# Down basis of a spline FFN in float32 on column halves of TensorE, with GpSimd rounding and a new order of the batch loop

## The chip, the cores and the metric

The kernel runs on one core of a Trainium2 chip. The metric is the device time of one execution in microseconds (us). PE is TensorE (the matrix engine), ACT ScalarE, DVE VectorE, POOL GpSimd, SP SyncE, which issues the DMAs. PE writes its products to eight PSUM banks of 128 x 512 float32.

## The reference, cut to what matters

Four batches, 512 tokens, width 512. Cross attention adds to x; then a gated FFN, whose three weight matrices are Catmull-Rom splines of few control points, adds to the result.

```python
# attention (per batch)
query, key = features @ Wq.T + bq, features @ Wk.T + bk
attention = softmax(query @ key.T)
x = x + layernorm(x) @ attention.T          # layernorm over the last axis
# FFN (per batch), INTER = 2048 rows
h = layernorm(x)
inter = silu(h @ gate_w.T) * (h @ up_w.T)
x = x + inter @ down_w.T                    # weights: spline_reconstruct(control points)
```

## The kernel before, in words

**Weights.** A spline matrix is, over most of its area, a smooth function, so each product with a weight matrix is split in two: a small basis part through nodes, and a residual with the breaks. For the down matrix the basis part is: `zd = d_u^T inter`, 128 node rows by 512 tokens, and then `zd` times `d_v` (the node weights). The residual is `d_r`, 16 tiles of 128 x 192 columns in blocks, times the rounded activations `ih`. The 2048 inner rows lie in 16 tiles m of 128; tile m = 4w + a touches only the node rows of class w.

**Precision.** PE takes float32r operands (rounded) in one pass and float32 in two recorded passes that are slower. To keep the precision of the basis product in float32r, both factors are split into a rounded part and a remainder: `d_u` is [P, 16, 2, 128] with high and low part, and an activation tile is `ih` (rounded, by ACT) and `il` (remainder, by POOL). Three products per tile (lines 1301, 1302, 1304) give `zd`.

**Order.** Every engine runs the same written list of stage calls (`attention_only`, then `ffn`), each with its own body for each stage, in strict order; semaphores join the engines. `ffn(b, a)` runs the FFN of batch b with the attention of batch a = b + 1 woven in; it is the body of a loop of three iterations, and then it runs once more for the last batch with no attention. The steps of a batch:

- `project`: basis coefficients `zg` of the normalised input (PE line 1273, ACT 775, DVE 950), and POOL's copy `xres` (line 1096).
- `gate_up(m)`: four products of 512 columns (lines 1287, 1289) into gbank[m % 2] and ubank[m % 2]. The gate part waits until tile m-2's SiLU has read its bank, the up part until its multiply has.
- `activate(m)`: ACT SiLU into one of three `inter` buffers (line 784), DVE multiply by the up result (line 958).
- `round_inter(m)`: ACT rounds `inter` to `ih[m]` (line 788), POOL computes `il` (line 1108).
- `down_basis(m)`: the three products above, accumulated in `zdbank`.
- `down(t, tiles)`: `ih[m]` times `d_r[m]` for 128 tokens (line 1318), 16 products for each of four t; `down_split` splits `zd` (ACT 795, DVE 968); `down_tail(t)`: `zd` times `d_v` (line 1325); DVE adds to `xres` (line 976), SP stores.
- attention of a: `qk` (PE 1150, float32; ACT 682), `energy(t)` (PE 1161, float32), `softmax(t)` (DVE maximum 849, ACT exp 694), `scale` (DVE reciprocal 853, four scalings 856), `prob_t(t)` (PE transposes 1204, all four need the scaled rows), `split_prob(t)` (ACT 714, DVE 879), `split_x` (ACT `xh` 720, DVE `xl` 883), `xm(t)` (PE 1247 to 1249, 12 products each), `add_xm`, `cast_t`, `norm_t` (PE 1262).

The energies and exps of the four row blocks stand together in the middle of the gate_up steps, after `activate` 8 and 9, and `down_basis` steps of earlier tiles stand between gate_up steps. SiLU and exp are in different ACT table sets; the compiler puts an ACT_TABLE_LOAD before the first function of another set. The prologue builds the weights; there `down_factors` splits the basis (ACT 748, DVE 923), POOL clears `d_u` (line 991), and `down_nodes` makes `d_v` (POOL 1055, DVE 896 to 901). In the prologue `node_weights` runs float32 products on strips of 32 rows (line 1225).

Of the kernel before, what the change touches and what calls it, by code (L numbers as in the profile page):

```python
# [49 lines left out]
LAG = 3  # L50
EARLY, FILL = 10, 3
HALF = 64
WIDTH = PERIOD / 4
# [77 lines left out]
def constants():  # L131
# [52 lines left out]
    at["d_node"] = np.repeat(idx[:, None], 2, 1).transpose(0, 1, 3, 2).reshape(P, 4, HID)  # L184
    c["d_coef"] = taps.transpose(0, 2, 3, 1).reshape(P, 4 * HID).astype(np.float32)
# [8 lines left out]
    for m in range(MT):  # L194
        w = m // CLS
        full, k = basis_at(tiles[m].astype(float), edges)
        at_cell = 8 * np.arange(D_LIVE // 4)[:, None] + 2 * w + np.arange(4)
        basis[:, m] = np.pad(full, ((0, 0), (0, 8)))[:, at_cell.ravel()]
# [15 lines left out]
def xattn_spline_ffn_kernel(nc: bass.Bass, d, out: bass.AP):  # L214
# [4 lines left out]
    with ctx:  # L219
# [18 lines left out]
        d_u = sb("d_u", [P, MT, 2, P], f32r)  # L238
# [40 lines left out]
        basis_f = sb("basis_f", [P, MT, D_LIVE], f32, prep)  # L279
# [12 lines left out]
        inter = sb("inter", [P, 3, TOK], f32)  # L292
        il = sb("il", [P, 2, TOK], f32r)
# [22 lines left out]
        def live(part, w):  # L316

            first, n = 2 * w, 16 if w + 1 < CLS else 15
            row = d_u[:, CLS * w:CLS * (w + 1), part]
            if w + 1 < CLS:  # L320
                return row.rearrange("p m (q e) -> p m q e", e=8)[:, :, :, first:first + 4]
            return row[:, :, first:first + 8 * n].rearrange("p m (q e) -> p m q e", e=8)[:, :, :, 0:4]

        def live_basis(w):

            n = 16 if w + 1 < CLS else 15
            return basis_f[:, CLS * w:CLS * (w + 1), 0:4 * n].rearrange("p m (q e) -> p m q e", e=4)

        def in_tiles(psum):
# [4 lines left out]
        zgbank, zdbank = bank[4], bank[5]  # L334
        abank = bank[6:8]
# [3 lines left out]
            consts_set warm_set du_zero win_hi win_split power_done node_mm node_hi node_done  # L339
            jump_sums jump_k2 jump_c jump_d jump_hi jump_split res_mm res_mul res_done  # L340
            dtap_mul dtap_sum dv_hi dv_done du_hi du_done
# [3 lines left out]
            x1_kept zg_mm zg_hi zg_done g_mm u_mm silu_done mult_done ih_done il_done zd_mm zd_hi zd_done  # L345
# [10 lines left out]
        def attention_only(st):  # L356
# [55 lines left out]
            st.down_factors()  # L412
# [44 lines left out]
        def ffn(st, b, a=None):  # L457

            st.project(b)
            for m in range(2):  # L460
                st.activate(b, m)
            st.round_inter(b, 0)
            st.activate(b, 2)
            st.round_inter(b, 1)
            st.activate(b, 3)
            st.round_inter(b, 2)
            if a is not None:
                st.qk(a)
            st.gate_up(b, 0)
            st.activate(b, 4)  # L470
            st.gate_up(b, 1)
            st.round_inter(b, 3)
            st.gate_up(b, 2)
            st.activate(b, 5)
            st.gate_up(b, 3)
            for m in range(4, 6):
                st.round_inter(b, m)
            st.down_basis(b, 0)
            st.activate(b, 6)
            for m in range(4, 6):  # L480
                st.gate_up(b, m)
            st.down_basis(b, 1)
            st.activate(b, 7)
            st.down_basis(b, 2)
            st.gate_up(b, 6)
            st.round_inter(b, 6)
            st.down_basis(b, 3)
            st.round_inter(b, 7)
            st.gate_up(b, 7)
            for m in range(8, 10):  # L490
                st.activate(b, m)
            st.down_basis(b, 4)
            st.gate_up(b, 8)
            if a is not None:
                for t in range(2):
                    st.softmax(a, t)
            st.round_inter(b, 8)
            st.gate_up(b, 9)
            if a is not None:
                st.energy(a, 0)  # L500
            st.round_inter(b, 9)
            if a is not None:
                st.softmax(a, 2)
                st.energy(a, 1)
                st.softmax(a, 3)
                st.scale(a)
            for m in range(5, 7):
                st.down_basis(b, m)
            st.activate(b, 10)
            if a is not None:  # L510
                st.energy(a, 2)
            st.activate(b, 11)
            if a is not None:
                st.split_prob(a, 0)
                st.energy(a, 3)
            st.down_basis(b, 7)
            st.gate_up(b, 10)
            st.down_basis(b, 8)
            st.gate_up(b, 11)
            st.down_basis(b, 9)  # L520
            st.round_inter(b, 10)
            if a is not None:
                st.prob_t(a, 0)
            st.gate_up(b, 12)
            if a is not None:
                st.prob_t(a, 1)
            st.gate_up(b, 13)
            st.activate(b, 12)
            if a is not None:
                st.prob_t(a, 2)  # L530
            st.down_basis(b, 10)
            st.gate_up(b, 14)
            if a is not None:
                st.prob_t(a, 3)
            st.gate_up(b, 15)
            if a is not None:
                st.split_prob(a, 1)
            st.down_basis(b, 11)
            st.round_inter(b, 11)
            st.down(b, 0, range(0, 13))  # L540
            st.activate(b, 13)
            if a is not None:
                st.split_prob(a, 2)
            st.round_inter(b, 12)
            for m in range(12, 14):
                st.down_basis(b, m)
            st.down(b, 0, range(13, 16))
            st.down(b, 1, range(0, 16))
            st.round_inter(b, 13)
            st.activate(b, 14)  # L550
            if a is not None:
                st.split_prob(a, 3)
                st.xm(a, 0)
            st.activate(b, 15)
            if a is not None:
                st.split_x(a)
            for m in range(14, 16):
                st.round_inter(b, m)
            if a is not None:
                st.stats(a)  # L560
            st.down_basis(b, 14)
            if a is not None:
                st.xm(a, 1)
            st.down_basis(b, 15)
            if a is not None:
# [36 lines left out]
        def _(sp):  # L602
# [24 lines left out]
            load(basis_f[:].rearrange("p m n -> p (m n)"), "d_basis", "dbasis_in")  # L627
# [35 lines left out]
        def _(act):  # L663
            class Stages:
# [104 lines left out]
                def project(b):  # L769
                    act.wait_ge(s["zg_mm"], b + 1)  # L770
                    if isinstance(b, int) and b == 0 or not isinstance(b, int):
                        act.wait_ge(s["res_done"], RES)
                        act.wait_ge(s["du_done"], CLS)
# [16 lines left out]
                def down_basis(b, m):  # L790
                    pass
# [568 lines left out]
```

## Time and profile before

| | |
|---|---|
| median of three runs | 295.74 us (295.48 to 298.01) |
| profiled execution, its span | 295.4 us |
| PE busy | 278.2 us (94%) |
| DVE, POOL, ACT busy | 179.8, 157.8, 153.9 us |
| chain that ended last, PE's share | 81% |
| DMA moved | 23.34 MB, mean 79 GB/s |

Matmuls are pipelined: a recorded duration (0.39 us for 512 columns) is longer than the distance from one start to the next (0.23 us). Distances between starts tell what PE can do.

### The profile page before, as it was taken

How to read it: one execution, taken by the hardware profiler on the slowest of the kernel's cores; microseconds unless marked ns; L12 is line 12 of the kernel's file. 1: busy time of each engine (PE TensorE's matmuls, PEld its weight loads, DVE VectorE, ACT ScalarE, POOL GpSimd, SP SyncE). 2: the span in 40 equal slices, each digit the busy share in tenths (PEclk: the TensorE clock that was granted, in tenths of full speed). 3: DMA queues.
4: the chain of work that ended last, by engine and by line, in shares of the span. 5: the costliest groups of instructions: out<-in, count | busy, mean ns of one | idle time of the engine just before them, and what ended most of it. 6: DMA issues, size and time to landing. Idle time of an engine off the chain costs nothing.

```text
span 295.4 us, 4068 instructions
## 1 busy us (share of the span) xinstructions
PE 278.2 (94%) x1298; PEld 199.5 (68%) x1300; DVE 179.8 (61%) x318; ACT 153.9 (52%) x259; POOL 157.8 (53%) x139
## 2 busy tenths in 40 slices
PE   8699489899999999999999999999999999799995
PEld 3132157654777888946868888657688888477894
DVE  1697988985466676743467856524677577343403
ACT  3044733224888923256899422458897132376710
POOL 5589252778565772225855723058547521598630
PEclk9958869999999999999999999999999999999999
DMA  7997044000900000036200000333000001100003
GB/s 204 376 426 290 0 124 163 0 2 0 354 3 0 3 0 2 21 121 237 118 0 0 0 0 0 142 118 166 0 0 0 0 0 71 71 0 3 0 0 144
DMA packets 7212, 23.34 MB, mean 79 GB/s; under 512 B 1185, under 2 KB 2337, under 8 KB 5793
## 3 DMA queue, kind: packets, MB, share of 16 engines
q1 hardware_dynamic: 7200, 23.20, 21.1%
q8 instruction: 6, 0.10, 0.1%
q14 instruction: 6, 0.04, 0.0%
HBM read 19.01 MB, written 4.19 MB: 79 GB/s over the span
## 4 chain that ended last, share of the span: by engine, by line
PE 81%; DVE 10%; DMA 2%; ACT 2%; POOL 2%; issue 1%; SPq 1%; DVEq 0%; POOLq 0%
PE bank L1287 11%; PE bank L1289 10%; PE bank L1318 10%; PE bank L1150 6%; PE bank L1304 5%; PE bank L1273 5%; PE bank L1301 5%; PE bank L1302 5%; PE bank L1325 4%; PE bank L1247 4%; PE bank L1248 4%; PE bank L1249 4%; PE bank L1161 3%; PE bank L1204 3%; DVE prod L872 2%; DMA power<-in_g_power 2%
## 5 line engine op out<-in xcount | busy, mean ns | idle before, releaser
L1108 POOL TENSOR_TENSOR il<-inter,ih 128x512 fp32r<-128x512 f32 x64 | 86.6, 1366 | 46.3 <-ACT ih L788 29.4
L958 DVE TENSOR_TENSOR inter<-inter,bank 128x512 f32<-128x512 f32 x64 | 43.6, 685 | 45.6 <-ACT inter L784 45.5
L784 ACT ACTIVATE inter<-bank 128x512 f32<-128x512 f32 x64 | 37.9, 596 | 17.0 <-PE bank L1289 14.4
L788 ACT ACTIVATE ih<-inter 128x512 fp32r<-128x512 f32 x64 | 39.3, 629 | 2.4 <-DVE inter L958 2.3
L759 ACT ACTIVATE qk<-bank,nmr,rstd 128x512 f32<-128x512 f32 x16 | 12.5, 779 | 40.0 <-PE bank L1249 22.5
L1318 PEld LDWEIGHTS bank<-d_r,ih 128*128 128x128 f32 x256 | 30.8, 191 | 2.1 <-ACT ih L788 1.0
L1318 PE MATMUL bank<-d_r,ih 128*128 128x192 f32 x256 | 31.1, 274 | 0.0
L1287 PE MATMUL bank<-xh,gate_r 128*128 128x512 f32 x64 | 27.3, 426 | 1.5 <-DVE zg L950 1.5
L1301 PE MATMUL bank<-ih,d_u 128*128 128x512 f32 x64 | 28.0, 437 | 0.0
L1096 POOL TENSOR_TENSOR xres<-x,ones 128x2048 f32<-128x2048 f32 x4 | 14.4, 3600 | 23.9 <-DMA out<-xres 23.6
L1287 PE MATMUL bank<-xh,up_r 128*128 128x512 f32 x64 | 25.6, 400 | 0.0
L1304 PE MATMUL bank<-il,d_u 128*128 128x512 f32 x64 | 25.2, 394 | 0.4 <-POOL il L1108 0.4
L1289 PE MATMUL bank<-zg,gate_v 102*128 102x512 f32 x64 | 25.4, 396 | 0.0
L1289 PE MATMUL bank<-zg,up_v 102*128 102x512 f32 x64 | 25.3, 395 | 0.0
L1247 PE MATMUL bank<-ph,xh 128*128 128x512 f32 x64 | 25.2, 394 | 0.0
L1302 PE MATMUL bank<-ih,d_u 128*128 128x512 f32 x64 | 25.2, 394 | 0.0
L1248 PE MATMUL bank<-pl,xh 128*128 128x512 f32 x64 | 24.9, 390 | 0.0
L1249 PE MATMUL bank<-ph,xl 128*128 128x512 f32 x64 | 24.9, 389 | 0.0
L1079 POOL TENSOR_TENSOR ve<-mv,eps 128x1 f32<-128x1 f32 x16 | 5.9, 369 | 33.7 <-DVE mv L935 33.7
L764 ACT ACTIVATE prob<-bank 128x512 f32<-128x512 f32 x16 | 8.7, 596 | 21.6 <-PE bank L1262 21.6
L1150 PE MATMUL bank<-ctxT,wqk 128*128 128x512 f32 x32 | 17.5, 696 | 0.0
L930 DVE TENSOR_TENSOR x<-x,qk 128x512 f32<-128x512 f32 x16 | 11.1, 694 | 9.7 <-ACT qk L759 9.7
(97 smaller groups left out, 519.3 us busy)
## 6 DMA issues: line engine op xcount, KB each, us to landing
x<-in_x SPq DMA_DIRECT2D x4, 1024.0 KB, 4.7
xT<-in_xT SPq DMA_DIRECT2D x4, 1024.0 KB, 7.0
out<-xres SPq DMA_DIRECT2D x16, 256.0 KB, 2.1
ctxT<-in_ctxT SPq DMA_DIRECT2D x4, 512.0 KB, 7.4
rd<-in_d_r SPq DMA_DIRECT2D x2, 768.0 KB, 6.2
knots<-in_d_knot SPq DMA_DIRECT2D x1, 1280.0 KB, 11.6
d_coef<-in_d_coef SPq DMA_DIRECT2D x1, 1024.0 KB, 14.9
d_pt<-in_d_node SPq DMA_DIRECT2D x1, 1024.0 KB, 17.5
```

The costliest lines, as they stand in the source:

```text
L784: nc.scalar.activation(inter[:, m % 3], gbank[m % 2][:], ACT.Silu).then_inc(s["silu_done"], 1)
L788: nc.scalar.activation(ih[:, m], inter[:, m % 3], ACT.Copy).then_inc(s["ih_done"], 1)
L958: V.tensor_tensor(inter[:, m % 3], inter[:, m % 3], ubank[m % 2][:], ALU.mult).then_inc(s["mult_done"], 1)
L1108: G.tensor_tensor(il[:, m % 2], inter[:, m % 3], ih[:, m].bitcast(f32), ALU.subtract).then_inc(s["il_done"], 1)
L1247: mm(abank[t % 2][:], xh[:, n, c], ph[:, n], start=n == 0, stop=False)
L1248: mm(abank[t % 2][:], xh[:, n, c], pl[:, n], start=False, stop=False)
L1287: mm(dst[m % 2][:], gu_r[n][:, a, w * P:(w + 1) * P], xn2r[:, a], start=True, stop=False)
L1289: mm(dst[m % 2][:], gu_v[n][:, m], zg[:], start=False, stop=True).then_inc(s[done], 1)
L1301: mm(zdbank[:], d_u[:, m, 0], ih[:, m], start=m == 0, stop=False)
L1302: mm(zdbank[:], d_u[:, m, 1], ih[:, m], start=False, stop=False)
L1304: mm(zdbank[:], d_u[:, m, 0], il[:, m % 2], start=False, stop=m == MT - 1).then_inc(s["zd_mm"], 1)
L1318: mm(in_blocks(obank[t][:], m // CLS), ih[:, m, t * P:(t + 1) * P], d_r[:, m], start=m == 0, stop=False, skip_group_check=True)
```

## The change

The down basis product is done in float32. `d_u` holds, for each tile, only the 64 node columns that the tile's class touches (two quarters of 32 rows). The node rows are permuted so that a class's nodes lie in one quarter. Tiles are taken in a new `ORDER`; consecutive tiles are of classes whose 64 columns go to the two halves of PE's columns, and so to PSUM partitions 0 to 63 and 64 to 127. The products run in two groups of eight tiles. The first group's result (classes 1 and 3) lies turned by 32 rows; it is copied and split (`odd_split`) and added in place by two products with a turned identity (`odd_place`). The remainder `il`, ACT's rounding, the split of `d_u` and its clearing go; POOL rounds the activations by a multiply with ones. `inter` holds all 16 tiles. The order of `ffn` is written anew.

```diff
-        d_u = sb("d_u", [P, MT, 2, P], f32r)
+        d_u = sb("d_u", [P, MT, D_LIVE], f32)
+        turn = sb("turn", [P, P], f32r)
-        inter = sb("inter", [P, 3, TOK], f32)
-        il = sb("il", [P, 2, TOK], f32r)
+        inter = sb("inter", [P, MT, TOK], f32)
+ORDER = [CLS * w + a for pair in ((1, 3), (0, 2)) for a in range(CLS) for w in pair]
+GROUP = 8
 # ACT
-                def down_factors():
-                    act.wait_ge(s["dbasis_in"], 16)
-                    act.wait_ge(s["du_zero"], 1)
-                    for w in range(CLS):
-                        nc.scalar.activation(live(0, w), live_basis(w), ACT.Copy).then_inc(s["du_hi"], 1)
+                def turn():
+                    act.wait_ge(s["ident_in"], 16)
+                    nc.scalar.activation(turn_[:, QUAD:P], ident[:, 0:P - QUAD], ACT.Copy).then_inc(s["turn_set"], 1)
+                    nc.scalar.activation(turn_[:, 0:QUAD], ident[:, P - QUAD:P], ACT.Copy).then_inc(s["turn_set"], 1)
                 def activate(b, m):
                     act.wait_ge(s["g_mm"], MT * b + m + 1)
-                    if m >= 3:
-                        act.wait_ge(s["il_done"], MT * b + m - 2)
-                    nc.scalar.activation(inter[:, m % 3], gbank[m % 2][:], ACT.Silu).then_inc(s["silu_done"], 1)
+                    nc.scalar.activation(inter[:, m], gbank[m % 2][:], ACT.Silu).then_inc(s["silu_done"], 1)
                 def round_inter(b, m):
-                    act.wait_ge(s["mult_done"], MT * b + m + 1)
-                    nc.scalar.activation(ih[:, m], inter[:, m % 3], ACT.Copy).then_inc(s["ih_done"], 1)
+                    pass
+                def odd_split(b):
+                    act.wait_ge(s["basis_mm"], 2 * b + 1)
+                    nc.scalar.activation(zd[:, 0], zgbank[:], ACT.Copy).then_inc(s["odd_hi"], 1)
 # DVE
+                def odd_split(b):
+                    dve.wait_ge(s["odd_hi"], b + 1)
+                    V.tensor_tensor(zd[:, 1], zgbank[:], zd[:, 0].bitcast(f32), ALU.subtract).then_inc(s["odd_done"], 1)
 # POOL
                 def round_inter(b, m):
-                    pool.wait_ge(s["ih_done"], MT * b + m + 1)
-                    if m >= 2:
-                        pool.wait_ge(s["zd_mm"], MT * b + m - 1)
-                    G.tensor_tensor(il[:, m % 2], inter[:, m % 3], ih[:, m].bitcast(f32), ALU.subtract).then_inc(s["il_done"], 1)
+                    pool.wait_ge(s["mult_done"], MT * b + m + 1)
+                    G.tensor_tensor(ih[:, m], inter[:, m], ones[:, 0].broadcast_to([P, TOK]), ALU.mult).then_inc(s["ih_done"], 1)
 # PE
-                def down_basis(b, m):
-                    if m == 0:
+                def down_basis(b, g):
+                    if g == 0:
+                        pe.wait_ge(s["dbasis_in"], 16)
+                    if g == 1:
                         pe.wait_ge(s["zd_done"], b)
-                    pe.wait_ge(s["ih_done"], MT * b + m + 1)
-                    mm(zdbank[:], d_u[:, m, 0], ih[:, m], start=m == 0, stop=False)
-                    mm(zdbank[:], d_u[:, m, 1], ih[:, m], start=False, stop=False)
-                    pe.wait_ge(s["il_done"], MT * b + m + 1)
-                    mm(zdbank[:], d_u[:, m, 0], il[:, m % 2], start=False, stop=m == MT - 1).then_inc(s["zd_mm"], 1)
+                    pe.wait_ge(s["mult_done"], MT * b + GROUP * (g + 1))
+                    dst = basis_bank[g]
+                    for m in range(GROUP * g, GROUP * (g + 1)):
+                        half = slice(m % 2 * HALF, (m % 2 + 1) * HALF)
+                        last = mm(dst[half], d_u[:, ORDER[m]], inter[:, m], start=m % (MT // 2) < 2, stop=g == 0 and m >= GROUP - 2, skip_group_check=True)
+                    last.then_inc(s["basis_mm"], 1)
+                def odd_place(b):
+                    pe.wait_ge(s["turn_set"], 2)
+                    pe.wait_ge(s["odd_done"], b + 1)
+                    for z in range(2):
+                        last = mm(zdbank[:], turn_[:], zd[:, z], start=False, stop=z == 1, skip_group_check=True)
+                    last.then_inc(s["odd_mm"], 1)
```

The new order of `ffn` (lines `if a is not None` left out; everything on `a` is attention):

```python
st.project(b)
for m in range(4): st.activate(b, m)
st.qk(a)
for m in range(4): st.gate_up(b, m)
for m in range(4): st.round_inter(b, m)
for m in range(4, 6): st.activate(b, m); st.gate_up(b, m)
for m in range(6, 8): st.activate(b, m); st.gate_up(b, m); st.round_inter(b, m - 2)
for m in range(8, 10):
    st.activate(b, m); st.gate_up(b, m); st.round_inter(b, m - 2)
    st.energy(a, m - 8); st.softmax(a, m - 8)
st.down_basis(b, 0)
for m in range(10, 12):
    st.activate(b, m); st.gate_up(b, m); st.round_inter(b, m - 2)
    st.energy(a, m - 8); st.softmax(a, m - 8)
st.odd_split(b)
st.scale(a)
for m in range(12, 14): st.activate(b, m); st.gate_up(b, m); st.round_inter(b, m - 2)
for m in range(14, 16):
    st.prob_t(a, m - 14); st.activate(b, m); st.gate_up(b, m); st.round_inter(b, m - 2)
st.split_prob(a, 0)
st.down(b, 0, range(0, 13))
st.prob_t(a, 2); st.split_prob(a, 1)
st.down_basis(b, 1)
st.odd_place(b)
for m in range(14, 16): st.round_inter(b, m)
st.prob_t(a, 3)
st.down(b, 0, range(13, 16))
st.split_prob(a, 2)
st.down(b, 1, range(0, 16))
st.split_prob(a, 3); st.split_x(a)
st.xm(a, 0); st.stats(a); st.xm(a, 1); st.xm(a, 2)
# from here on as before: mean_shift, add_xm, down_split, xm 3, down 2, down_tail, down 3, norm_t
```

## Rows read from the trace of the kernel before

**Rows 1.** The page's first table: busy us (share of the span) xinstructions
```profile
PE 278.2 (94%) x1298; PEld 199.5 (68%) x1300; DVE 179.8 (61%) x318; ACT 153.9 (52%) x259; POOL 157.8 (53%) x139
```
**Rows 2.** Busy time by stage: stretch, us, busy by engine, granted clock (PEclk), DMA
```profile
66.00:127.00 61.00, 60.99 (x296) 46.74 (x293) 38.20 (x69) 36.49 (x61) 33.45 (x30) 1.00 0.14 53
```
**Rows 3.** The chain of waits in order of time: start us, us, what
```profile
119.29 1.76 PE bank L1318 x16
...
131.07 3.43 PE bank L1150 x8
...
192.40 3.43 PE bank L1150 x8
```
**Rows 4.** Timeline of PE, second iteration: start us, us, engine, line, tile
```profile
134.58 0.39 PE L1287 MATMUL bank<-xh,up_r 128*128 128x512 f32 x1
...
135.75 0.40 PE L1289 MATMUL bank<-zg,gate_v 102*128 102x512 f32 x1
...
136.62 0.50 PE L1287 MATMUL bank<-xh,up_r 128*128 128x512 f32 x1
...
137.43 0.40 PE L1287 MATMUL bank<-xh,gate_r 128*128 128x512 f32 x1
...
138.36 0.40 PE L1301 MATMUL bank<-ih,d_u 128*128 128x512 f32 x1
...
139.06 0.40 PE L1287 MATMUL bank<-xh,gate_r 128*128 128x512 f32 x1
```
**Rows 5.** Timeline of ACT and DVE, second iteration, tile 1
```profile
136.18 0.60 ACT L784 ACTIVATE inter<-bank 128x512 f32<-128x512 f32 x1 [0.33 <-PE bank L1289]
...
136.81 0.69 DVE L958 TENSOR_TENSOR inter<-inter,bank 128x512 f32<-128x512 f32 x1 [0.24 <-ACT inter L784]
```
**Rows 6.** Timeline of PE in the prologue, node_weights 3 and 4
```profile
25.33 1.11 PE L1225 MATMUL bank<-weighted,coef 32*102 32x512 f32 x4
```
**Rows 7.** Groups by line of POOL: busy us, mean ns of one, idle before
```profile
L1108 POOL TENSOR_TENSOR il<-inter,ih 128x512 fp32r<-128x512 f32 x64 | 86.6, 1366 | 46.3 <-ACT ih L788 29.4 <-PE bank L1304 16.4
L1096 POOL TENSOR_TENSOR xres<-x,ones 128x2048 f32<-128x2048 f32 x4 | 14.4, 3600 | 23.9 <-DMA out<-xres 23.6 <-POOL d_r L1033 0.3
```
**Rows 8.** Timeline of DVE and POOL in the prologue
```profile
44.66 2.64 DVE L923 TENSOR_TENSOR d_u<-basis_f,d_u 128x256 fp32r<-128x256 f32 x4
...
41.18 5.18 POOL L1055 TENSOR_TENSOR d_coef<-d_coef,d_pt 128x512 f32<-128x512 f32 x4
```
**Rows 9.** Timeline of ACT around the exps, first iteration
```profile
86.71 1.28 ACT L694 ACT_TABLE_LOAD   x1
...
91.84 0.69 ACT L694 ACTIVATE prob<-bank,nmax 128x512 f32<-128x512 f32 x1
...
92.64 1.28 ACT L784 ACT_TABLE_LOAD   x1
93.93 1.09 ACT L784 ACTIVATE inter<-bank 128x512 f32<-128x512 f32 x2
```
**Rows 10.** Timeline of DVE in the same stretch: maxima and scalings
```profile
87.33 1.38 DVE L849 TENSOR_REDUCE nmax<-bank 128x1 f32<-128x512 f32 x2
...
92.86 1.82 DVE L856 TENSOR_SCALAR prob<-prob,rinv 128x512 f32<-128x512 f32 x4
```
**Rows 11.** Timeline of ACT and DVE, the split of x, first iteration
```profile
101.65 1.91 ACT L720 ACTIVATE xh<-xT 128x2048 fp32r<-128x2048 f32 x1
...
103.59 2.29 DVE L883 TENSOR_TENSOR xl<-xT,xh 128x2048 fp32r<-128x2048 f32 x1 [0.97 <-ACT xh L720]
```
**Rows 12.** Timeline of PE in the prologue, after its longest idle time
```profile
36.90 0.80 PE L1194 MATMUL bank<-knots,spread 128*128 128x192 bf16 x4 [3.56 <-DVE knots L918]
```
**Rows 13.** Busy time by stage in the prologue, columns as in rows 2
```profile
34.50:35.00 0.50, 0.00 (x0) 0.00 (x0) 0.41 (x2) 0.29 (x1) 0.00 (x0) 0.97 0.00 0
...
41.50:42.00 0.50, 0.28 (x2) 0.17 (x2) 0.50 (x2) 0.00 (x0) 0.50 (x1) 0.70 0.87 319
...
18.70:25.30 6.60, 6.60 (x9) 2.52 (x8) 6.50 (x12) 3.08 (x3) 5.50 (x5) 0.54 1.02 412
```

More of the change, by code:

```diff
@@ L196, in constants @@
         full, k = basis_at(tiles[m].astype(float), edges)
-        at_cell = 8 * np.arange(D_LIVE // 4)[:, None] + 2 * w + np.arange(4)
-        basis[:, m] = np.pad(full, ((0, 0), (0, 8)))[:, at_cell.ravel()]
+        placed = np.zeros((P, P))
+        placed[:, row.ravel()] = full
+        basis[:, m] = np.concatenate([placed[:, QUAD * q:QUAD * (q + 1)] for q in (w, (w + 1) % CLS)], 1)
         if not np.isclose(basis[:, m].sum(), full.sum()):
@@ L474, in ffn @@
[L474 to L475 removed]
+            for m in range(4):
+                st.gate_up(b, m)
+            for m in range(4):
+                st.round_inter(b, m)
             for m in range(4, 6):
[L477 to L480, printed above, removed]
+                st.activate(b, m)
                 st.gate_up(b, m)
[L482 to L483 removed]
@@ L484, in ffn @@
[L484 to L489, printed above, removed]
+            for m in range(6, 8):
+                st.activate(b, m)
+                st.gate_up(b, m)
+                st.round_inter(b, m - 2)
             for m in range(8, 10):
                 st.activate(b, m)
-            st.down_basis(b, 4)
-            st.gate_up(b, 8)
-            if a is not None:
-                for t in range(2):
-                    st.softmax(a, t)
@@ L497, in ffn @@
[L497 to L505, printed above, removed]
-                st.scale(a)
[L507 to L512, printed above, removed]
+                st.gate_up(b, m)
@@ new lines, in ffn @@
+                st.round_inter(b, m - 2)
+                if a is not None:
+                    st.energy(a, m - 8)
+                    st.softmax(a, m - 8)
+            st.down_basis(b, 0)
+            for m in range(10, 12):
+                st.activate(b, m)
+                st.gate_up(b, m)
+                st.round_inter(b, m - 2)
+                if a is not None:
+                    st.energy(a, m - 8)
+                    st.softmax(a, m - 8)
+            st.odd_split(b)
+            if a is not None:
+                st.scale(a)
@@ L513, in ffn @@
+            for m in range(12, 14):
+                st.activate(b, m)
+                st.gate_up(b, m)
+                st.round_inter(b, m - 2)
+            for m in range(14, 16):
+                if a is not None:
+                    st.prob_t(a, m - 14)
+                st.activate(b, m)
+                st.gate_up(b, m)
+                st.round_inter(b, m - 2)
             if a is not None:
                 st.split_prob(a, 0)
-                st.energy(a, 3)
-            st.down_basis(b, 7)
@@ L517, in ffn @@
[L517 to L528, printed above, removed]
+            st.down(b, 0, range(0, 13))
             if a is not None:
                 st.prob_t(a, 2)
-            st.down_basis(b, 10)
@@ L532, in ffn @@
[L532 to L536, printed above, removed]
-                st.split_prob(a, 1)
[L538 to L556, printed above, removed]
+                st.split_prob(a, 1)
+            st.down_basis(b, 1)
+            st.odd_place(b)
             for m in range(14, 16):
@@ L559, in ffn @@
             if a is not None:
+                st.prob_t(a, 3)
+            st.down(b, 0, range(13, 16))
+            if a is not None:
+                st.split_prob(a, 2)
+            st.down(b, 1, range(0, 16))
+            if a is not None:
+                st.split_prob(a, 3)
+                st.split_x(a)
+                st.xm(a, 0)
                 st.stats(a)
-            st.down_basis(b, 14)
-            if a is not None:
                 st.xm(a, 1)
-            st.down_basis(b, 15)
-            if a is not None:
                 st.xm(a, 2)
```

89 lines of the change are left out of this document (40 added, 49 removed).

## The prediction

> **What bounds it now.** I read the page's first table, then the stages, then one iteration's timeline. TensorE (PE) is busy for 94% of the span [rows 1]; over the 61 us of the first loop iteration it is busy 60.99 us at a granted clock of 1.00 [rows 2]. One iteration is 192.40 - 131.07 = 61.33 us in the chain of waits [rows 3], and the chain is PE instructions nearly throughout. So a PE microsecond removed is a microsecond gained, but any wait that the new order opens on PE is paid in full. ScalarE, VectorE and GpSimd are each about half busy; their waits cost nothing today because the written order puts basis products of old tiles (0.70 us each) between gate_up steps.
>
> **Unit costs.** A gate_up step (four products of 512 columns) is 138.36 - 137.43 = 0.93 us of PE, a tile's three basis products 139.06 - 138.36 = 0.70 us, one product 0.23 us [rows 4]. A float32 product of 512 columns is recorded as two passes; eight passes take 3.43 us [rows 3], 0.43 us a pass, 0.86 us a product. SiLU starts 136.18 - 135.75 = 0.43 us after the last gate product does, takes 0.60, and the multiply takes 0.69 [rows 4, 5]. Two successive steps that wait only for each other's banks run at 136.62 - 134.58 = 2.04 us a pair and not 1.87 [rows 4]; since the gate_v product then starts late as well, I take 2.1.
>
> **Basis products.** Removed: 16 tiles x 0.70 = 11.2 us of PE per batch. Added: 16 float32 products on 64 columns, two groups of eight. One after the other a group is 8 x 2 x 0.43 = 6.9 us; if the two halves run at the same time, 3.45. The trace has no product on a column half. The nearest rows: two float32 products on different row strips (node_weights 3 and 4), four passes, take 1.11 us with their fill [rows 6], against 4 x 0.43 = 1.72 and more in sequence. So separate strips do overlap, float32 included. A half also asks for moving data at the rate of a 0.43 us pass; two at once ask for what one 0.23 us product already gets. I take overlap with 0.25 us for entering and leaving: 3.7 us a group; bounds 3.5 and 7.1. Added too: two products for odd_place, 0.5 us. Net PE work: -11.2 + 7.4 + 0.5 = -3.3 us per batch.
>
> The Trainium skill (TensorEngine Tiling (Array Packing), Key Properties and Performance Considerations) says that column tiles work in parallel, up to twofold at 64 columns, and that a change of tiling mode drains the engine. The trace shows only the row form. By the page's factor the two groups would be 6.9 us, without it 13.8.
>
> **Other removals.** ScalarE loses 64 roundings, VectorE nothing per tile. GpSimd rounds instead of subtracting: 1.37 us is the present two-input subtraction, 3.60 / 4 = 0.90 the multiply by broadcast ones per 512 elements [rows 7]. Even 1.37 x 16 = 22 us lies inside the 61 us iteration, and the rounding of tile 12 is done before down needs it; I cost it at nothing. In the prologue VectorE's d_u work, 2.64 us from 44.66, is on the chain, but GpSimd's d_coef products, which the next VectorE step needs, end only at 41.18 + 5.18 = 46.36 [rows 8]: gain 47.3 - 46.4 = 0.9 us. The two small `turn` copies lie on an idle ScalarE. No DMA grows.
>
> **The new order, tiles 0 to 7.** No basis product stands between them now: four pairs at 2.1 instead of 1.87 lose 0.9 us, and the two qk evictions (full tiles like SiLU's, so 0.6 each or more) now stand ahead of SiLU 4 and delay it by about 0.7. About 0.2 us of this exists today: tile 2 already waits. I take +1.4.
>
> **Tiles 8 to 15: SiLU and exp alternate.** This decides. Today the four exps stand together: one table load before them (86.71) and one after (92.64), each 1.28 us, and the next activation starts at 93.93 at once [rows 9]. Now ScalarE runs SiLU 8, exp 0, SiLU 9, exp 1, SiLU 10, exp 2, SiLU 11, exp 3: eight loads instead of two. VectorE alternates too: multiply, maximum (0.69 each, [rows 5, 10]), and exp t waits for the maximum behind multiply 8+t. With exp and its read-out 0.80 us (91.84 to 92.64) a round is SiLU 0.60, then load against multiply plus maximum (1.45 with the gaps), 0.80, load 1.30: 4.15 us. PE needs 0.93 + 0.86 = 1.79 for the same tile. Counted from the start of gate_up 8:
> SiLU 8 at 0.9, exp 0 ends 3.75; SiLU 9 at 5.1, exp 1 ends 7.9; SiLU 10 at 9.2, exp 2 ends 12.05; SiLU 11 at 13.35 to 13.95, multiply 11 to 14.7, maximum 3 to 15.4, exp 3 to 16.2.
> Then odd_split stands ahead of scale: copy to 16.8, subtraction to 17.5, reciprocal 0.2 (today 92.86 - 92.64 from the last exp's end to the first scaling), four scalings 1.82 [rows 10] to 19.5; only behind them multiply 12, to 20.2.
> PE meanwhile: gate_up 8, 9 and energy 0, 1 to 3.6, down_basis 0 to 7.3, tiles 10 and 11 with energies to 10.9, gate_up 12 to 11.8. gate_up 13 needs multiply 11 and ends at 15.4 instead of 12.8; prob_t 0 needs all four scalings, 19.5; gate_up 14 needs multiply 12, so gate_up 15 ends at 22.2. Unhindered it would be 15.6 (prob_t at an estimated 0.4, from 0.11 per 192-column product of 1.76 / 16 [rows 3]). Stall: 6.6 us per iteration. DMA and POOL queues lose nothing by it.
>
> **Behind tile 15.** prob_t 2 needs split_prob 1, which stands behind SiLU 15: 0.6 us. And prob_t 3 now stands behind down_basis 1. After it come PE's drain and eviction 3 (0.2 + 0.6, as long as SiLU), xh 1.91 and xl 2.29 [rows 11], 5.0 us, before xm 0 may start; PE has three and sixteen down products, 19 x 0.11 = 2.1 us, for cover. Today more than 5 us of products cover the same chain. Stall: 2.9 us. From xm 0 on, the order is the old one less two basis triples.
>
> **Sum at full clock.** Iteration: 61.3 - 3.3 + 1.4 + 6.6 + 0.6 + 2.9 = 69.5, +8.2, times three = +24.6. The last batch has no softmax beside it; -3.3 of work, +0.5 net of paired-step stalls (up to seven pairs at +0.2, less the waits for il that go), -2.8. Prologue -0.9. 295.4 + 24.6 - 2.8 - 0.9 = 316.3.
>
> **The clock.** PE stood for 3.56 us before it resumed at 36.90 [rows 12], so from 33.34; the granted clock fell just before 35.0 and came back near 41.7, 4.8 us after the restart; another low stretch held through more than 6 us of busy PE [rows 13]. These are the two levels, 1.2 and 2.4 GHz. The new stalls (4.1 us of emptiness before prob_t 0 and 2.9 before xm 0) are longer than the 1.6 us after which it fell there. 4.8 us at half rate lose 2.4 us; the first loss absorbs the 0.6 us wait: 1.8 + 2.4 = 4.2 per iteration. Bounds 0 and 2 x 3.3, from the 6.6 us. As the work after both stalls is dense full-array products, I take 3.0: +9. That gives 325.3; the median shown, 295.74, stands 0.3 over the profiled span, so 326.
>
> **Rivals.** *Waits without a fall of the clock*: 317. For: the falls of the trace are in the prologue, with thin work around them; here the PE is dense before and after. Against: both new stalls last longer than 1.6 us. 0.18.
> *The halves run one after the other*: each group 7.1 instead of 3.7. Of group 0's 3.4 us, 1.0 is hidden by the ScalarE chain (SiLU 10 waits at 11.6 instead of 9.2), group 1's is paid: +5.8 x 3 + 6.8 = +24, 350. Against: two strips overlap in [rows 6]; for: those are row strips, not column halves. 0.13.
> *Not slower: the softmax chain is covered.* If scale ends before PE gets to prob_t 0, the 6.6 us and the clock losses go: 316.3 - 19.8 + 0.3 = 297; it decides once the softmax stall is under about 0.5 us. For: ScalarE is only half busy on average. Against: the in-order chain above needs 19.5 us where PE brings 12.8. If the xm wait is covered as well: 288. Together 0.09.
> *Each table load holds ScalarE as long again.* Seven loads stand before scale: 7 x 1.28 x 3 = +27, 353. Against: the exp-to-SiLU switch in [rows 9] shows no more than the load. 0.02. The Trainium skill (ScalarE: Activation LUTs, What ACT_TABLE_LOAD costs) states such an extra, a drain of about 1.38 us per switch; the trace disagrees.
>
> **Numbers.** Forecast 0.58. Range 308 to 342: the forecast with its clock and overlap bounds and the no-fall rival, about 0.8. A measurement here tells 1% from no change. Faster by over 1% 0.04, within 1% 0.05 (both from the covered case), slower 0.91.
>
> **What would show it.** ScalarE: 8 table loads per iteration in the exp/SiLU stretch where two stood. PE: a wait of about 4 us before L1204's first transposes ended by VectorE's prob scaling, one of about 3 us before L1247 ended by xl, low clock after one or both. Group: eight products in about 3.7 us, starts of even and odd tiles together; iteration near 72 to 73 us. Wrong if the group takes 7, if the loads are fewer, or if PE does not wait at prob_t 0.

## The result and the profile after

The changed kernel takes 328.43 us (median of four runs, 327.81 to 329.1) where the one before takes 296.0 in the runs beside it: a ratio of 1.1076, 95% interval 1.1035 to 1.1117. The forecast was 326. The profiled execution has a span of 326.6 us at a mean granted clock of 0.92; before it was 295.4 at 0.969.

First, the page's first table of the changed kernel, with the row of the granted clock in 40 slices (beside [rows 1]):

```profile
PE 285.7 (87%) x1244; PEld 182.2 (56%) x1244; DVE 178.9 (55%) x318; ACT 146.1 (45%) x215; POOL 132.7 (41%) x138
...
PEclk9969699999996979999987979999976969999999
```

Every engine's share fell. PE's microseconds rose although it has 54 instructions fewer: part of them ran at half rate, the dips of the clock row. The chain of waits gives the ledger (start us, us, what; as [rows 3]). `project` (L1234) opens each iteration:

```profile
64.98 3.46 PE bank L1234 x8
...
84.41 1.28 ACT L731
...
110.41 0.66 PE bank L1279 x2
...
112.04 1.92 ACT xh L672
113.98 2.30 DVE xl L836
...
137.23 3.68 PE bank L1234 x8
...
209.30 3.68 PE bank L1234 x8
...
283.47 3.69 PE bank L1234 x8
```

The same rows of the kernel before:

```profile
66.29 3.46 PE bank L1273 x8
...
127.40 3.68 PE bank L1273 x8
...
188.72 3.68 PE bank L1273 x8
...
250.08 3.69 PE bank L1273 x8
```

`project` starts at 64.98, 137.23, 209.30 and 283.47; before, at 66.29, 127.40, 188.72 and 250.08. So up to the first one the kernel is 1.3 us faster. The three iterations take 72.25, 72.07 and 74.17 instead of 61.11, 61.32 and 61.36: +34.7. The last batch, 43.1 instead of 45.3, is 2.2 faster. Sum: +31.2, the difference of the spans. And the chain now goes over table loads (ACT L731) and over the splitting of x (L672, L836), where [rows 3] had PE.

What stops PE is in its timeline, first iteration, rows with idle time in brackets and those that date the steps (start us, us, line, tile):

```profile
80.49 0.40 PE L1248 MATMUL bank<-xh,gate_r 128*128 128x512 f32 x1
...
84.44 3.65 PE L1268 MATMUL bank<-inter,d_u 128*64 128x512 f32 x16
88.03 0.50 PE L1248 MATMUL bank<-xh,gate_r 128*128 128x512 f32 x1
...
94.45 0.50 PE L1248 MATMUL bank<-xh,gate_r 128*128 128x512 f32 x1 [1.64 <-ACT inter L731]
...
99.59 1.11 PE L1165 MATMUL bank<-masks,prob 128*128 128x128 f32 x4 [3.46 <-DVE prob L809]
...
106.17 0.66 PE L1165 MATMUL bank<-masks,prob 128*128 128x128 f32 x4 [0.35 <-DVE pl L832]
...
116.33 0.50 PE L1208 MATMUL bank<-ph,xh 128*128 128x512 f32 x1 [2.71 <-DVE xl L836]
```

The waits foreseen are all there: before gate_up 13 (L1248 at 94.45), before the first transposes of `prob` (L1165), before prob_t 2, and before xm 0 (L1208). The group of eight down basis products (L1268) takes 88.03 - 84.44 = 3.6 us for 16 passes.

ScalarE in the stretch where SiLU (L731) and exp (L646) alternate:

```profile
81.66 0.60 ACT L731 ACTIVATE inter<-bank 128x512 f32<-128x512 f32 x1 [0.61 <-PE bank L1250]
82.28 1.28 ACT L646 ACT_TABLE_LOAD   x1
83.62 0.69 ACT L646 ACTIVATE prob<-bank,nmax 128x512 f32<-128x512 f32 x1
84.20 0.19 ACT L646 ACTIVATION_READ_ACCUMULATOR prob<-bank,nmax 128x1 f32 x1
84.41 1.28 ACT L731 ACT_TABLE_LOAD   x1
85.71 0.60 ACT L731 ACTIVATE inter<-bank 128x512 f32<-128x512 f32 x1
```

One round, SiLU to SiLU, is 85.71 - 81.66 = 4.05 us, and 2.56 of it are the two loads.

And the busy time by stage, around the places where the clock fell, in the first iteration and (last two rows) in the third (stretch, us, busy by engine, granted clock; as [rows 2]):

```profile
97.00:98.00 1.00, 0.00 (x0) 0.00 (x0) 0.92 (x3) 0.98 (x2) 0.00 (x0) 0.50 0.00 0
99.50:102.00 2.50, 2.41 (x8) 2.12 (x9) 1.23 (x3) 0.00 (x0) 1.79 (x2) 0.50 0.00 0
103.50:104.00 0.50, 0.50 (x4) 0.42 (x2) 0.00 (x0) 0.00 (x0) 0.50 (x1) 0.91 0.00 0
114.00:116.30 2.30, 0.00 (x0) 0.00 (x0) 2.30 (x2) 0.00 (x0) 0.00 (x0) 1.00 0.00 0
117.50:119.00 1.50, 1.50 (x5) 1.22 (x4) 1.40 (x6) 0.00 (x0) 0.00 (x0) 0.50 0.00 0
121.00:122.00 1.00, 1.00 (x6) 0.82 (x5) 0.20 (x1) 0.76 (x1) 0.00 (x0) 1.00 0.00 0
...
244.00:251.00 7.00, 6.91 (x27) 6.03 (x28) 3.20 (x7) 2.17 (x4) 3.59 (x4) 0.55 0.00 0
...
261.00:264.00 3.00, 2.67 (x6) 2.15 (x7) 2.90 (x9) 0.00 (x0) 0.00 (x0) 0.50 0.00 0
```

PE was busy at half rate from its restart at 99.59 to about 103.5, and again from about 117.25 to 120.7. The second fall came while PE was already at work again. In the third iteration both low stretches were longer: the clock was low until 250.4, 6.3 us after the restart at 244.09, and then from 260.6, still inside the wait before xm 0, until 267.4, 6.1 us after the restart at 261.33.

### The profile page after: what moved, and what is told of

Its sections match the earlier page's. It is cut to its first block, busy times and chain, and to the rows that moved or that the text cites. A ratio compares the mean times of both kernels' runs of the same rounds, so it can differ in the third digit from the quotient of the medians.

```text
span 326.6 us, 3809 instructions
## 1 busy us (share of the span) xinstructions
PE 285.7 (87%) x1244; PEld 182.2 (56%) x1244; DVE 178.9 (55%) x318; ACT 146.1 (45%) x215; POOL 132.7 (41%) x138
## 4 chain that ended last, share of the span: by engine, by line
PE 60%; DVE 14%; ACT 12%; issue 8%; DMA 2%; POOL 1%; SPq 1%; ACTq 0%; DVEq 0%; POOLq 0%
PE bank L1248 8%; PE bank L1250 6%; PE bank L1295 6%; PE bank L1268 5%; PE bank L1208 5%; PE bank L1111 5%; PE bank L1209 5%; PE bank L1210 4%; PE bank L1234 4%; PE bank L1165 4%; ACT inter L731 3%; DVE nmax L802 3%; PE bank L1302 3%; ACT L731 3%; DVE prod L825 2%
## 5 line engine op out<-in xcount | busy, mean ns | idle before, releaser
L1063 POOL TENSOR_TENSOR ih<-inter,ones 128x512 fp32r<-128x512 f32 x64 | 65.6, 1040 | 60.0 <-DVE inter L909 58.4
L731 ACT ACTIVATE inter<-bank 128x512 f32<-128x512 f32 x64 | 37.7, 598 | 40.3 <-PE bank L1250 40.0
L1248 PE MATMUL bank<-xh,gate_r 128*128 128x512 f32 x64 | 33.3, 520 | 6.4 <-ACT inter L731 4.9
L1208 PE MATMUL bank<-ph,xh 128*128 128x512 f32 x64 | 28.0, 437 | 8.1 <-DVE xl L836 8.1
L1248 PE MATMUL bank<-xh,up_r 128*128 128x512 f32 x64 | 28.5, 446 | 1.5 <-DVE inter L909 1.3
L1268 PE MATMUL bank<-inter,d_u 128*64 128x512 f32 x128 | 29.2, 598 | 0.0
L1165 PE MATMUL bank<-masks,prob 128*128 128x128 f32 x64 | 13.7, 362 | 11.9 <-DVE prob L809 11.2
L1248 PEld LDWEIGHTS bank<-xh,gate_r 128*128 128x128 f32 x64 | 12.8, 200 | 17.4 <-ACT inter L731 7.4
L1248 PEld LDWEIGHTS bank<-xh,up_r 128*128 128x128 f32 x64 | 12.7, 199 | 15.2 <-DVE inter L909 11.9
L1208 PEld LDWEIGHTS bank<-ph,xh 128*128 128x128 f32 x64 | 13.5, 211 | 11.8 <-DVE xl L836 8.7
L1165 PEld LDWEIGHTS bank<-masks,prob 128*128 128x128 f32 x64 | 10.8, 191 | 16.0 <-DVE prob L809 11.6
L832 DVE TENSOR_TENSOR pl<-bank,ph 128x512 fp32r<-128x512 f32 x16 | 10.6, 687 | 16.3 <-ACT ph L666 16.3
```

The costliest lines, as they stand in the source:

```text
L731: nc.scalar.activation(inter[:, m], gbank[m % 2][:], ACT.Silu).then_inc(s["silu_done"], 1)
L1063: G.tensor_tensor(ih[:, m], inter[:, m], ones[:, 0].broadcast_to([P, TOK]), ALU.mult).then_inc(s["ih_done"], 1)
L1165: last = nc.tensor.transpose(abank[t % 2][:, m * P:(m + 1) * P], prob[:, m, t * P:(t + 1) * P], ident)
L1208: mm(abank[t % 2][:], xh[:, n, c], ph[:, n], start=n == 0, stop=False)
L1248: mm(dst[m % 2][:], gu_r[n][:, a, w * P:(w + 1) * P], xn2r[:, a], start=True, stop=False)
L1268: last = mm(dst[half], d_u[:, ORDER[m]], inter[:, m], start=m % (MT // 2) < 2, stop=g == 0 and m >= GROUP - 2, skip_group_check=True)
```

## The experiments

The theory: the whole loss is order. The alternation of SiLU and exp makes the softmax late, prob_t 3 makes xm 0 late, and each of these PE waits costs again in clock; the float32 products on column halves are a gain. The rivals were that the halves run one after the other, that something other than these two waits is slow, and that the clock would fall without them. Each ratio below is against the kernel before on the same chip. The changed kernel itself was not run beside them, so what a run gives back is a difference of two medians taken apart; worked out from the ratios, such a difference comes out up to 1.4 us otherwise.

**No second table.** The loop's exps become Identity, which needs no table change: the trace has 7 loads in place of 31. The softmax values of this kernel are therefore wrong; its steps and tiles are the same.

```diff
-nc.scalar.activation(prob[:, t], abank[t % 2][:], ACT.Exp, bias=nmax[:, t:t + 1],
+func = ACT.Exp if isinstance(b, int) and b == 0 else ACT.Identity
+nc.scalar.activation(prob[:, t], abank[t % 2][:], func, bias=nmax[:, t:t + 1],
```

> In the loop's three iterations the softmax takes Identity in place of exp (its values are left wrong; same tiles, same read-out), so that no activation table changes there; the order stays. Theory A (the stall before prob_t 0 comes from the strictly alternating chain SiLU, multiply, maximum, exp, of which the table loads are only a part, since each exp load runs beside multiply and maximum): prob_t 0 comes 1.8 us earlier per iteration, 328.4 - 5.4 = 323 us, and a wait of over 1.5 us on the prob scaling stays. Rival B (the loads are the stall): 4 rounds shorter by 2.6 us each would take away the whole stall and its clock fall, 328.4 - 3 x (5.2 + 2.0) = 307 us.

Measured: 323.1 us, ratio 1.0923 [1.0877, 1.0969]. Of the 32.4 us lost, 5.3 came back. Timelines of ACT and PE of this kernel, first iteration:

```profile
84.74 0.69 ACT L647 ACTIVATE prob<-bank,nmax 128x512 f32<-128x512 f32 x1 [1.36 <-DVE nmax L803]
...
98.57 1.12 PE L1166 MATMUL bank<-masks,prob 128*128 128x128 f32 x4 [3.45 <-DVE prob L810]
```

Without any load, exp now waits 1.36 us for VectorE's maximum, which stands behind the multiply of the same tile. The waits at gate_up 13 are gone, the one before prob_t 0 is as long as before. So the loads are the smaller part. What remains is that ScalarE and VectorE, each in its written order, hand each tile to and fro.

**The scaling ahead of the split of the odd group.**

```diff
-st.odd_split(b)
 if a is not None: st.scale(a)
+st.odd_split(b)
```

> One edit: scale stands ahead of odd_split on VectorE and ScalarE. Theory A (prob_t 0 waits for the last scaling, which waits behind odd_split's copy and subtraction): the scalings start 1.1 us earlier, 328.4 - 3 x 1.1 = 325 us. Rival (multiply 12 or SiLU 12's table load sets the pace there, so nothing moves): 328 us.

Measured: 324.78 us, ratio 1.0981 [1.0932, 1.103]. PE's row before prob_t 0:

```profile
98.13 1.12 PE L1165 MATMUL bank<-masks,prob 128*128 128x128 f32 x4 [2.36 <-DVE prob L809]
```

The wait shrank from 3.46 to 2.36 us. Three times 1.1 is 3.3 of the 3.7 gained.

**prob_t 3 early.**

```diff
 st.prob_t(a, 2); st.split_prob(a, 1)
+st.prob_t(a, 3)
 st.down_basis(b, 1); st.odd_place(b)
 ...
-st.prob_t(a, 3)
```

> One edit: prob_t 3 stands directly behind prob_t 2, ahead of down_basis 1. Theory A (the wait before xm 0 comes from prob_t 3 standing late, and its eviction, xh and xl behind it; the clock fall in xm 0 comes from that wait): the 2.7 us wait and the fall (3.4 us at half rate, 1.7 us) both go, 328.4 - 3 x 4.4 = 315 us. Rival 1 (xm waits for something else too, such as the split of x alone): the wait stays above 1 us, 323 or more. Rival 2 (the clock falls there whatever PE does): 328.4 - 3 x 2.7 = 320 us.

Measured: 314.35 us, ratio 1.0636 [1.0583, 1.069]. Busy time by stage over the place of the old wait:

```profile
104.00:118.00 14.00, 13.66 (x80) 9.72 (x79) 8.90 (x16) 5.35 (x7) 2.73 (x4) 1.00 0.00 1
```

No wait before xm 0 and no second fall, in any of the three iterations. The move of one step gives back 14.1 us. By the starts of `project` the iterations are 4.5, 4.0 and 6.0 us shorter: 2.7 is the wait itself, and the rest fits the clock behind it, 1.7 in the first two (half of the 3.4 us at half rate) and 3.0 in the third (half of 6.1).

**The halves in turn.** Within a group, one half's four tiles first, then the other's.

```diff
-for m in range(GROUP * g, GROUP * (g + 1)):
+for m in [GROUP * g + n for n in (0, 2, 4, 6, 1, 3, 5, 7)]:
```

> One edit: in each group of eight the four tiles of one column half run first, then the four of the other, instead of in turns. The work and the result are the same. Theory A (products on the two halves run at the same time only because neighbours in the order lie on different halves): a group takes 6.9 us instead of 3.6; of group 0's 3.3 us about 2.5 reach the ScalarE chain, group 1's are paid: 328.4 + 3 x 5.8 + 6.6 = 352 us. Rival (the engine takes a later product of the free half ahead, or a 64-column float32 product is cheap by itself): groups stay at 3.6 us, 328 us.

Measured: 338.45 us, ratio 1.1462 [1.1407, 1.1518], between the two expectations. PE's timeline of this kernel, the group whole and then two of its stretches by themselves:

```profile
84.90 5.42 PE L1268 MATMUL bank<-inter,d_u 128*64 128x512 f32 x16
...
86.24 0.59 PE L1268 MATMUL bank<-inter,d_u 128*64 128x512 f32 x1
...
86.67 0.65 PE L1268 MATMUL bank<-inter,d_u 128*64 128x512 f32 x2
```

The passes start singly at 84.90, 85.39, 85.81 and 86.24, two at a time from 86.67 until 88.0, and singly again from 88.45 to 89.73. The records do not name the half, but passes on one half lie 0.43 us apart, so those that start beside another must be the other half's. So the two halves do run at once, and a pass takes 0.43 us alone or in a pair. But the overlap reached only about four passes ahead in the written order: eight passes on one half leave four alone at each end, 5.4 us and not 6.9 or 3.6. Eight groups longer by 1.8 us make 14.7, and 10.0 show. Part of it lay under the ScalarE chain (the wait at gate_up 13 is 0.92 instead of 1.64 us), and the clock cost less: in the first iteration it stayed at 1.00 behind the same wait before xm 0 (this wait, then busy time by stage behind it):

```profile
119.27 0.50 PE L1208 MATMUL bank<-ph,xh 128*128 128x512 f32 x1 [2.71 <-DVE xl L836]
```
```profile
119.20:130.00 10.80, 10.73 (x47) 8.91 (x48) 8.07 (x20) 2.83 (x4) 3.25 (x6) 1.00 0.01 2
```

The Trainium skill (TensorE: Matmul & The Clock Gate, Part 3: Packing small matmuls) has the products start and end strictly in their written order. By the starts recorded here this does not hold between column halves: products of the second half started while some of the first half, written earlier, had not.

**Fillers in place of the waits.** Products whose result is not used run in the loop ahead of each waiting step, so that PE is never empty; nothing on the chain gets earlier.

```diff
 def prob_t(b, t):
+    if t == 0 and not (isinstance(b, int) and b == 0):
+        for _ in range(14): mm(zdbank[:], gu_r[0][:, 0, 0:P], xn2r[:, 0], start=True, stop=True)
 def xm(b, t):
+    if t == 0 and not (isinstance(b, int) and b == 0):
+        for _ in range(11): mm(zgbank[:], gu_r[0][:, 0, 0:P], ih[:, MT - 1], start=True, stop=True)
 def gate_up(b, m):
+    if m == 13 and not isinstance(b, int):
+        for _ in range(7): mm(zdbank[:], gu_r[0][:, 0, 0:P], xn2r[:, 0], start=True, stop=True)
```

> Added work only: in the loop PE runs products whose result nobody reads while it would wait: 7 of 512 columns ahead of gate_up 13, 14 ahead of prob_t 0, 11 ahead of xm 0 (0.23 us each, a little under the waits they fill). Theory A (the waits let the granted clock fall, and the work behind each then runs at half rate for 3.4 to 4 us): the waits stay as long, the clock stays at 1.00, 328.4 - 3 x (2.0 + 1.7) = 317 us. Rival (the half-rate stretches only take up time in which PE would have waited anyway, so filling gains nothing): 328 us or a little more.

Measured: 315.74 us, ratio 1.066 [1.0617, 1.0703]. More work in PE, 12.7 us less time. Stage and PE row of this kernel:

```profile
67.00:137.00 70.00, 68.73 (x314) 46.38 (x313) 36.93 (x67) 38.94 (x54) 25.88 (x28) 1.00 0.14 53
...
98.67 0.66 PE L1168 MATMUL bank<-masks,prob 128*128 128x128 f32 x4 [0.26 <-DVE prob L809]
```

The clock stays at 1.00. The iterations are 68.8, 68.95 and 68.94, so what the clock cost was 3.5, 3.1 and 5.2 us of them. The remaining 7.6 us over the 61.3 of before are order at full clock, less what the new basis saves. The changed kernel's longer third iteration (74.17) is gone here too, so it was clock: both low stretches in it were longer.

**The exps together.** Exps 0 and 1, then down_basis 0, exps 2 and 3, scaling right behind, and only then tiles 10 and 11: two table loads instead of eight.

```diff
     # in the loop over m = 8, 9
-        st.softmax(a, m - 8)
+for t in range(2): st.softmax(a, t)
 st.down_basis(b, 0)
+for t in range(2, 4): st.energy(a, t); st.softmax(a, t)
+st.scale(a)
 for m in range(10, 12):
     st.activate(b, m); st.gate_up(b, m); st.round_inter(b, m - 2)
-    st.energy(a, m - 8); st.softmax(a, m - 8)
 st.odd_split(b)
-st.scale(a)
```

> The order of the exp stretch: SiLU 8 and 9, then all four energies and exps around down_basis 0, scale directly behind them, then tiles 10 and on; two table loads instead of eight. Theory A: exp 3 ends about 10.6 us after gate_up 8 starts and scaling about 12.5, so prob_t 0 no longer waits; SiLU 10 waits for ScalarE's table load (11.9), which leaves PE a wait of about 2.3 us ahead of gate_up 12; the clock fall there goes. 328.4 - 3 x (4.3 + 2.0) = 309 us. Rival (the chain's length is that of exps and scaling themselves, wherever they stand): 322 us or more.

Measured: 312.05 us, ratio 1.0529 [1.0486, 1.0571]: 16.4 us back. PE's rows with the longest waits of this kernel:

```profile
93.04 0.49 PE L1250 MATMUL bank<-xh,gate_r 128*128 128x512 f32 x1 [1.64 <-ACT inter L733]
...
110.34 0.80 PE L1210 MATMUL bank<-ph,xh 128*128 128x512 f32 x1 [2.71 <-DVE xl L838]
```

No wait is left at prob_t 0, but a wait of 1.64 us is now at gate_up 12: tiles 10 and 11 stand behind all exps and scalings. It was expected, at 2.3 us. Not expected was the clock behind it. In the first iteration it stayed at 1.00; in the second and third it fell 1.4 us after the restart, for 3.4 us. Busy time by stage in the second:

```profile
161.30:164.50 3.20, 3.20 (x11) 2.58 (x10) 1.69 (x3) 1.14 (x2) 2.52 (x4) 0.50 0.00 0
```

Those two falls lose 1.7 us each, and the iterations show it: 66.5, 68.3 and 68.3. This is the larger part of the 3 us that are missing from the 19 expected.

**Both moves**, the exps together and prob_t 3 early:

> The new order of the exp stretch (as in the kernel with the exps together) and prob_t 3 ahead of down_basis 1, both. Theory A (the two waits are independent): the second move is worth again the 14 us that it was worth alone (328.4 - 314.4), 312.1 - 14.1 = 298 us. Rival (once the first wait is gone PE comes sooner to the second chain, which is then longer exposed): 301 us or more.

Measured: 299.11 us, ratio 1.011 [1.0068, 1.0152]. Two moved steps take back 29.3 of 32.4 us. The iterations are 62.3, 64.06 and 62.5. In the second one the clock fell at 157.7, after waits of 1.63 and 0.22 us. The same waits left it at 1.00 in the other two. A stretch behind that fall:

```profile
158.00:159.00 1.00, 1.00 (x5) 0.70 (x4) 0.61 (x1) 0.48 (x1) 0.90 (x2) 0.50 0.00 0
```

**An order woven anew.** The same products, put so that each in-order engine finds its inputs ready: qk in two parts, energies 0 and 1 between tiles 5 and 8, the exps two and two around down_basis 0, which runs as two blocks of four tiles, prob_t 0 to 3 behind tiles 11 to 14, down_basis 1 late:

```diff
+qk(a, 0); tiles 0-2; qk(a, 1); tiles 3-5; energy 0; tiles 6-7; maximum 0; energy 1
+tile 8; maximum 1; tile 9; exps 0, 1; down_basis 0 (first four)
+energies, maxima and exps 2, 3; scale; down_basis 0 (last four); tiles 10-11
+prob_t 0; tile 12; prob_t 1; tile 13; prob_t 2; tile 14; prob_t 3; tile 15; split_x; odd_split
+down 0 (13 tiles); down_basis 1; down 0 (3); down 1; odd_place; xm 0
```

> The changed kernel's basis (float32, column halves, GpSimd rounding) in an order woven for it: qk in two parts, energies 0 and 1 between gate_up steps, exps together with down_basis 0 in two halves around energies 2 and 3, scaling while ScalarE reloads its table, prob_t between gate_up 11 and 15, odd_split behind the split of x, odd_place ahead of xm 0. Theory A (the slowdown is the order's waits and clock falls, and the basis itself saves 3.3 us of PE per batch): an iteration near 59 us, 285 us in all, faster than the kernel before by 3 to 4%. Rival (float32 halves, GpSimd's rounding or the turned identity cost something that the waits hid): 290 us or more.

Measured: 292.48 us, ratio 0.9876 [0.9842, 0.991]: faster than the kernel before, but 7.5 over the 285 expected. The number alone would fit the rival (290 or more), so the rows have to tell. The iterations are 60.6 to 60.9 us. Rows of the chain of this kernel, then of PE's timeline:

```profile
71.53 0.78 ACT L752
...
89.93 1.87 PE bank L1300 x8
```
```profile
87.94 1.98 PE L1150 MATMUL bank<-qk 128*128 128x512 f32 x4 [0.68 <-ACT prob L667]
...
134.29 0.49 PE L1279 MATMUL bank<-xh,gate_r 128*128 128x512 f32 x1 [0.90 <-ACT inter L752]
```

The first qk eviction, written before the first SiLU, ended at 71.5, and only then did the SiLU table load start: part of it (0.78 us from 71.53) is on the chain. There are 0.68 us before energy 2, which waits for exp 0, 0.56 before gate_up 0 in the first iteration, and 0.90 before gate_up 2, which waits for SiLU 0, in the other two. My sum had left out these new waits and the paired-step losses. The iterations, expected at 59, make 5.2 of the 7.5 us; the other 2.3 were not separated.

**The woven order with the halves in turn** inside its blocks:

> The same woven order, but within each block of basis products one column half's tiles run first, then the other's. Theory C, formed from the kernel with the halves in turn (PE starts products of the other half while up to four passes of the first are still open): blocks of four tiles (two per half, four passes) still overlap wholly; only the block of eight loses 1.8 us per batch, 7 us in all over the woven kernel. Rival (that kernel's 5.4 us came from cheaper 64-column passes, 0.33 us each in sequence, and not from overlap across the order): the blocks of four take 2.7 instead of 1.9 us too, 12 us or more over the woven kernel.

Measured: 299.8 us, ratio 1.012 [1.0086, 1.0154], 7.3 slower than the order it is made from (7 expected). The chain of this kernel, a block of four tiles and a group of eight:

```profile
90.21 1.87 PE bank L1300 x8
...
101.06 5.35 PE bank L1300 x16
```

The block, four passes of one half and then four of the other, takes 1.87 us as it did in pairs. The group of eight takes 5.35, and 3.58 in pairs: 1.8 us in each of the four batches. That is what a reach of about four passes makes of them.

**The first qk eviction behind SiLU 0 and 1:**

```diff
+act(0); act(1)
 st.qk(a, 0)
-act(0); gu(0); act(1); gu(1)
+gu(0); gu(1)
```

> As the woven kernel, but the first qk eviction stands behind SiLU 0 and 1 on ScalarE, no longer ahead of the table load for SiLU 0. Theory A (of the 60.8 us an iteration takes, about 1.2 us is SiLU 0 waiting for that eviction and the load behind it): 292.5 - 3 x 1.2 = 289 us. Rival (the second gate_up pair waits for its multiply anyway): 292 us.

Measured: 289.47 us, ratio 0.9765 [0.9732, 0.9799], the fastest version. Its chain, `project`:

```profile
125.39 3.68 PE bank L1268 x8
...
184.86 3.68 PE bank L1268 x8
...
244.31 3.69 PE bank L1268 x8
```

An iteration is 59.5 us, 1.9 less than before the change, with the same float32 products as the changed kernel: the slowdown was the order, not the new work. The wait of 0.90 us before gate_up 2 is gone. Nearly 0.7 us before energy 2 remains.

## Why the prediction was right

**Unit costs and basis.** The group took 3.58 us (3.7 taken, 6.9 to 7.1 the rival); `odd_place` 0.66 (0.5). The last batch gained 2.2 (2.8), the prologue 1.3 (0.9). The halves run at once; the halves-serial rival is excluded by 3.58 us and by the two kernels with the halves in turn, whose groups of eight are each 1.8 us longer.

**Tiles 0 to 7.** PE took up gate_up 0 at 71.7 (0.23 before its second product at 71.94) and gate_up 8 at 80.49: 8.8 us where eight steps of 0.93 make 7.4. Loss 1.35 (1.4).

**Exp stretch.** Counted from gate_up 8 in the first iteration, exp 3 ended after 16.0 us (16.2) and prob_t 0 started after 19.1 (19.5), behind a wait of 3.46 (about 4.1). gate_up 15 ended after 23.7, of which 2.0 is clock: 21.7 at full clock (22.2). There are 8 loads an iteration in this stretch, 1283 ns each, where [rows 9] has two. The next activation starts 0.01 to 0.06 us behind each of them, so the rival with the double price is out.

**Behind tile 15.** The wait for split_prob 1 was 0.35 (0.6), in a stretch just after the low clock; that before xm 0 was 2.71 (2.9). Taking the second away gave 14.1 us, as its working says: wait and fall together.

**Sum at full clock.** The fillers show it nearly bare: 68.9 us an iteration (69.5 predicted). The exp stretch, the groups and the waits behind tile 15 came out smaller than taken, `odd_place` larger, about 1.0 together; the 0.4 between that and the 0.6 was not separated.

**Clock.** The step that was least sure: 3.0 us an iteration taken, bounds 0 and 6.6. Seen are 2.0 and 1.7 in the first iteration, and the fillers put the whole at 3.5, 3.1 and 5.2. The direction was right and the first term (1.8) too. The second was taken at 2.4 from a fall that lasts 4.8 us after the restart [rows 12, 13]. Here low clock lasted 3.4 in two iterations; in the third, both stretches held for more than 6 us after the restart, and nothing in my working told that. The terms as first added up, 4.2 an iteration, come near the measured 3.9 on average. The step down to 3.0, for the dense products behind both waits, rested on no row of low clock behind dense work, and went the wrong way. So over three iterations the clock cost 11.8 us and not 9: +2.8. The full-clock part was 1.7 less, the last batch and the prologue together 0.2 more. That is the 1.3 us between the forecast's 325.3 and the span of 326.6; the other 1.1 lie around the span. The median stands 1.8 over it, and I took 0.3 and rounded up by 0.4. The 0.3 set the median of three executions against the span of one; in every execution of the kernel before that has both on record, the time stands 1.8 to 2.1 over the span. The rival without a fall was priced rightly: the fillers, without one, make 315.7 of its 317.

**The covered case.** It needed a softmax stall under about 0.5 us. The kernel had over 5. The kernel with both moves is that case built: 299.1, with 288 forecast for both waits covered. It came out 11 higher, since waits of 1.85 us moved to gate_up 12 (5.6 over three iterations) and one clock fall came of them (1.7). Another 2.1 is again the time around the span (2.4 against 0.3); the rest I did not separate. The 1.4 of tiles 0 to 7 stood in the 288 already.

**POOL's rounding.** Group by line, the changed kernel (beside [rows 7]):

```profile
L1063 POOL TENSOR_TENSOR ih<-inter,ones 128x512 fp32r<-128x512 f32 x64 | 65.6, 1040 | 60.0 <-DVE inter L909 58.4
```

It takes 1.04 us, inside the bounds 0.90 and 1.37, and waits only for VectorE. It costs nothing, as taken.

## What to carry to other kernels

When two in-order engines work at two streams, count one round of the alternation through both, table loads and hand-overs included, and compare it with what PE brings in that time. Loads are only part of it: here 5.3 us of a stretch worth 16.4. Where a step moves, list what stands behind it on other engines: one moved prob_t cost 14.1 us. And a PE wait of some 3 us can cost more than itself, since the clock may go down behind it: the 2.7 us before xm 0 cost 4.0 to 6.0 an iteration. It is not certain: the same 2.7 us cost nothing extra in one iteration of the kernel with the halves in turn, and waits of 1.63 + 0.22 us were followed by a fall in three of six iterations.

## What was not expected of the hardware

- Products on the free half of the columns started although products of the other half, written earlier, still waited: overlap reached about four passes ahead, so eight passes of each half in turn took 5.4 us where pairs take 3.6, but four of each took 1.87 either way.
- The clock can fall after PE has resumed: idle for 2.71 us, restart at 116.33, full clock until about 117.25, then half for 3.4 us. In the third iteration of the same kernel it fell inside that wait and stayed low for 6.1 us after the restart. It can also fall after a wait of only 1.64 + 0.22 us: it did in two of three iterations with the exps together and in one of three with both moves (1.7 us lost each time), and stayed at 1.00 in the others.
- Unused products in the place of waits made the kernel 12.7 us faster.
- Rounding by a multiply with a broadcast column of ones took GpSimd 1.04 us for 512 columns, against 1.37 for a subtraction of two full inputs.
